# Issuing the second copy of the high query rows on ScalarE's queue

## The reference

```python
def xattn(x, ctx, Wq, bq, Wk, Wv, Wo):        # both layers, in short
    q = (layernorm(x) @ Wq + bq).reshape(b, l, 16, 8)
    k = (ctx @ Wk).reshape(b, m, 16, 8)
    v = (ctx @ Wv).reshape(b, m, 16, 8)
    att = softmax(einsum('blhd,bmhd->blmh', q, k) / sqrt(8), axis=2)
    return einsum('blmh,bmhd->blhd', att, v).reshape(b, l, 128) @ Wo
x = x + xattn(...)                   # layer 0
x = x + quantised_ffn(layernorm(x))
x = x + xattn(...)                   # layer 1
x = x + experts(layernorm(x))        # 8 experts
```

## Time and profile before

| | |
|---|---|
| median of three runs | 409.39 us (409.24 to 411.62) |
| the profiled execution's own span | 411.6 us |
| TensorE matmuls busy | 309.9 us, 75% |
| VectorE busy | 267.8 us, 65% |
| ScalarE busy | 167.3 us, 41% |
| GpSimd busy | 91.0 us, 22% |
| DMA engines | 14.0% on the queue of SP, 0.3% on that of ScalarE |

### The profile page before, as it was taken

One profiled execution on the slowest core, in us unless ns is written; L12 is line 12 of the kernel. 1 busy time (PEld: TensorE's weight loads), 2 busy tenths in 40 slices (PEclk: granted clock), 3 DMA queues, 4 the chain that ended last, 5 costly groups with the idle time before them and its releaser, 6 DMA issues.

```text
span 411.6 us, 4782 instructions
## 1 busy us (share of the span) xinstructions
PE 309.9 (75%) x1455; PEld 184.4 (45%) x1455; DVE 267.8 (65%) x682; ACT 167.3 (41%) x261; POOL 91.0 (22%) x87
## 2 busy tenths in 40 slices
PE   0068689978888843712657698989889999999995
PEld 0046333343434431202234334444437868888883
DVE  1576555367663736985677734766348799988883
ACT  0232152333546313863112334554664445454542
POOL 1511037001010205931110700101010653330600
PEclk9999985589999965855555559999999999999999
DMA  4338421030000091030230200200000000000000
GB/s 143 88 65 175 105 58 28 6 77 2 6 4 5 15 236 40 0 103 2 58 91 7 60 21 14 71 6 2 7 0 2 1 2 25 2 1 25 2 25 25
DMA packets 15902, 16.53 MB, mean 40 GB/s; under 512 B 3435, under 2 KB 11804, under 8 KB 15878
## 3 DMA queue, kind: packets, MB, share of 16 engines
q1 hardware_dynamic: 14834, 13.71, 14.0%
q0 software_dynamic: 704, 2.12, 2.0%
q10 hardware_dynamic: 340, 0.40, 0.3%
HBM read 4.53 MB, written 1.05 MB: 14 GB/s over the span
## 4 chain that ended last, share of the span: by engine, by line
PE 58%; DVE 25%; DMA 6%; ACT 6%; issue 3%; POOL 1%; SPq 0%; ACTq 0%; DVEq 0%; POOLq 0%
PE ps_acc L1092 11%; PE ps_tok L941 6%; PE ps_key L950 5%; DVE mx L645 5%; DMA wkv<-in_wkv 5%; PE ps_acc L1062 4%; PE ps_acc L1064 3%; PE ps_acc L1063 3%; DVE xn L571 3%; DVE stats L561 3%; PE ps_m L958 2%; PE ps_m L980 2%; PE ps_tok L1049 2%; PE ps_tok L1051 2%; DVE axb L849 2%
## 5 line engine op out<-in xcount | busy, mean ns | idle before, releaser
L645 DVE TENSOR_REDUCE mx<-ps_tok 128x4 f32<-128x312 f32 x128 | 57.4, 477 | 38.3 <-PE ps_tok L941 37.4
L441 ACT ACTIVATE big<-ps_key 104x512 f32<-104x512 f32 x96 | 55.3, 596 | 54.1 <-PE ps_key L950 52.8
L941 PE MATMUL ps_tok<-kst,qst 97*128 97x312 f32 x128 | 59.0, 487 | 14.7 <-DVE mx L645 14.2
L334 POOL TENSOR_SCALAR veps<-mv 128x4 f32<-128x4 f32 x16 | 3.7, 229 | 247.8 <-DVE mv L564 247.8
L941 PEld LDWEIGHTS ps_tok<-kst,qst 97*128 97x128 f32 x128 | 30.8, 247 | 52.6 <-DVE mx L645 27.0
L950 PE MATMUL ps_key<-qst,kst 105*104 105x512 f32 x96 | 45.3, 483 | 3.9 <-ACT big L441 1.9
L787 DVE TENSOR_TENSOR qst<-big,qst 128x512 fp32r<-128x512 f32 x64 | 44.3, 692 | 2.2
L785 DVE CAST qst<-big 128x512 fp32r<-128x512 f32 x64 | 27.0, 422 | 9.7 <-ACT big L505 9.5
L571 DVE TENSOR_SCALAR xn<-x,mv,rstd 128x128 f32<-128x128 f32 x64 | 27.5, 595 | 8.8 <-POOL rstd L335 8.8
L505 ACT ACTIVATE big<-ps_tok,b 128x512 f32<-128x512 f32 x32 | 22.0, 689 | 25.1 <-PE ps_tok L1051 24.9
L1092 PE MATMUL ps_acc<-big,vbd 104*32 104x512 f32 x192 | 30.5, 712 | 0.7 <-ACT big L441 0.7
(11 more groups left out here) (192 smaller groups left out, 543.5 us busy)
## 6 DMA issues: line engine op xcount, KB each, us to landing
qst<-qhi SPq DMA_DIRECT2D x64, 64.0 KB, 2.0
kst<-rbuf SPq DMA_DIRECT2D x24, 156.0 KB, 3.0
qst<-qlo SPq DMA_DIRECT2D x32, 64.0 KB, 2.0
w1f<-in_w POOLq DMA_DIRECT2D x2, 1024.0 KB, 7.9
x<-in_x SPq DMA_DIRECT2D x4, 256.0 KB, 10.5
out<-xn SPq DMA_DIRECT2D x4, 256.0 KB, 2.3
qst<-mthl SPq DMA_DIRECT2D x32, 16.0 KB
wqo<-in_wqo SPq DMA_DIRECT2D x1, 256.0 KB, 7.1
```

The costliest lines, as they stand in the source:

```text
L441: act.activation(p[:, j, :], key[n % 2][0:PR, :], ACT.Exp, scale=SCALE).then_inc(q["p_ready"], 1)
L645: nc.vector.tensor_reduce(mx[:, u % 2, t, g, 0, :], tok[n % 2][:, 0:KG].rearrange("p (j h) -> p h j", h=HG), AX.X, ALU.max).then_inc(q["to ...
L941: mm(tok[n % 2][:, 0:KG], qst[0:MASKROW + 1, s, g, 128 * t:128 * t + 128], kst[0:MASKROW + 1, b, g, :], start=True, stop=True).then_inc(q[ ...
```

## The change

The copy of qhi to rows 64 to 95 of the stack is no longer issued by SP but by ScalarE, for all eight units, right behind the ACTIVATE that writes qhi. ScalarE first waits for its own semaphore `q_hi`, and from unit 3 on for `key_put`, as SP does. Sources, destinations, sizes and completion semaphores are the same; SP keeps eight of the twelve DMAs of a unit, ScalarE gets four.

```diff
--- before.py
+++ after.py
@@ -243,6 +243,8 @@
         FIRST_LOG, FIRST_A, FIRST_B, FIRST_C = 5, 6, 8, 12
 
 
+        SECOND_ON_ACT = range(2 * B)
+
         ACT_LATE = dict(copy=0.4, key=0.2)
         DVE_LATE = dict(on=0.1)
 
@@ -301,7 +303,8 @@
                             if u == 0 and g > 0:
                                 key_stack(g)
                             move(qst[0:32, s, g, :], qhi[r, u % 2, :], stack_q[u % 2][g])
-                            move(qst[64:96, s, g, :], qhi[r, u % 2, :], stack_q[u % 2][g])
+                            if u not in SECOND_ON_ACT:
+                                move(qst[64:96, s, g, :], qhi[r, u % 2, :], stack_q[u % 2][g])
                             if g == 0:
                                 sp.wait_ge(q["q_lo"], u + 1)
                             move(qst[32:64, s, g, :], qlo[r, u % 2, :], stack_q[u % 2][g])
@@ -460,6 +463,13 @@
                         if u == B:
                             act.wait_ge(q["const_set"], 5)
                         act.activation(qhi[:, u % 2, :], m1[:, :], ACT.Identity, bias=bq[:, L:L + 1]).then_inc(q["q_hi"], 1)
+                        if u in SECOND_ON_ACT:
+                            act.wait_ge(q["q_hi"], u + 1)
+                            if u >= 3:
+                                act.wait_ge(q["key_put"], 12 * (u - 2))
+                            for g in range(G):
+                                act.dma_start(qst[64:96, u % 3, g, :].bitcast(F32), qhi[32 * g:32 * g + 32, u % 2, :].bitcast(F32)
+                                              ).then_inc(stack_q[u % 2][g], 16)
                     if job == "ot":
                         act.wait_ge(q["ot_put"], u + 1)
                         if u >= 1:
```

## The result

| | before | after |
|---|---|---|
| median | 413.51 us (12 runs, 408.4 to 420.1) | 414.87 us (12 runs, 412.1 to 417.8) |
| ratio, 95% interval | | 1.0099, 1.0052 to 1.0146 |
| span of the profiled execution | 411.6 us | 416.0 us |

The account below looks back on a forecast made before the run. No queue and not ScalarE was taken as the bound; TensorE ended the chain for 58%, VectorE 25%. Costs 0.85 (unit 2) plus 1.3 (unit 7) gave 2.15 us, +0.5%: 409.39 became 411.5 us, range 408.8 to 418.2.

Parts of the forecast that it names:

- SP's relief: SP issues 32 fewer copies, a unit's stack out 2.5 us sooner; gain taken as 0 of at most 0.9 us.
- The price of an issue, 0.63 us: Each of four DMA issues behind qhi on ScalarE takes 0.63 us, blocking ScalarE 2.5 us per unit.
- Units 0, 1, 4 and 5 hidden: ScalarE idles behind qhi there, 4.11 us in unit 4 and longer in the others, so cost 0.
- Unit 2, +0.85 us: Delayed exponential moves a key matmul by 1.8 us; TensorE's idling takes up part, probability matmuls start 0.85 us later.
- Unit 3, 0: Key matmul waits for the delayed exponential, but TensorE had idled 2.46 us for VectorE's rounding of weights: cost 0.
- Unit 6, 0: Two key matmuls are delayed, but TensorE waits 2.92 us for VectorE's line 571 there anyway: cost 0.
- Unit 7, +1.3 us: Two key matmuls wait for delayed exponentials with no TensorE idle time behind them; probability matmuls move by 1.3 us.
- The sum, 2.15 us: Whole kernel: 0.85 us from unit 2 plus 1.3 from unit 7, all else 0; +0.5%.
- the clock apart as a rival: TensorE's clock falls behind unit 7's stall: 413 to 421 us, chance 0.12; unit 2's low stretch shortens: about 406, 0.08.
- the blocked queues: ScalarE's and SP's issues cannot overlap: 4.9 us blocked per unit, 8.75 us together, 418.1 us; chance 0.20.
- issues of 0.9 us or more: Sign on either queue, ScalarE's or SP's, that would make the rival of queues holding each other up.
- Hidden altogether: ScalarE's issues as short as 0.4 us, or unseen idle time eats the stalls: 409.4 us; chance 0.15.

Follow-up runs that it names:

- e8_covered_again: Repeat run of the kernel before with the second qhi copy moved to ScalarE's queue only in units 0, 1, 4 and 5; ratio 1.0003.
- e4_eight: Against the change: ScalarE issues both qhi copies, eight DMAs behind each qhi, and SP only those of qlo; ratio to the kernel before 1.0385.
- e1_covered: Kernel before with the second qhi copy moved to ScalarE's queue only in units 0, 1, 4 and 5; first run, ratio 1.0039.
- e3_late: Against the change: all eight units on ScalarE's queue, but issues of units 2, 3, 6, 7 placed behind exponentials two units earlier; ratio to the kernel before 0.9983.
- e10_only_seven: Kernel before with the second qhi copy moved to ScalarE's queue in unit 7 alone; ratio 1.0061.
- e6_two_seven: Kernel before with the second qhi copy moved to ScalarE's queue in units 2 and 7 alone; ratio 1.0124.
- e2_exposed: Kernel before with the second qhi copy moved to ScalarE's queue only in units 2, 3, 6 and 7; ratio 1.0037.
- e5_held: Kernel before, all DMAs on SP, with four dummy ScalarE writes behind qhi in units 2, 3, 6 and 7; ratio 1.0098.
- e9_only_two: Kernel before with the second qhi copy moved to ScalarE's queue in unit 2 alone; ratio 1.0040.
- e7_change_again: The change as it is, all eight units, measured again against the kernel before; ratio 1.0146.

## Why the prediction was right, and where it was off

- **SP's relief is worth nothing.** Right. The wait that bounded the gain went from 0.9 to 0.7 us, and SP's stack of the second unit, out 3.5 us earlier, made nobody start sooner: e8_covered_again, with the relief in units 0, 1, 4 and 5, is at 1.0003.
- **The price of an issue, 0.63 us.** Too low where both queues issue in step: in units 2 and 7 four took 2.88 us, 0.72 each, and the exponential started 2.95 us after qhi's end, not 2.5. The second and third are the long ones (0.87 and 0.76 us in unit 2). In unit 4, where SP's second issue started 0.4 us behind ScalarE's second instead of 0.2, four took 2.45 us, the price of the forecast, and so did the issues of e4_eight from unit 1 on. The term held for a queue that isn't disturbed; the disturbance, left to a rival, was there in part.
- **Units 0, 1, 4 and 5 hidden.** Right (e8_covered_again), up to 0.1 us in unit 0, whose four issues took 3.86 us.
- **Unit 2, +0.85 us.** Right in mechanism, mis-sized: 1.5 us. The table has pairs from 1.2 to 2.0; the cleanest are the profiles whose key matmuls there took 0.63 us, the time at 1.2 GHz, with 5.53 or 5.54 us without the hold-up (e1_covered, e3_late, e10_only_seven) and 6.99 with it (the change, e6_two_seven). The stall was 0.45 us longer, and the 1.70 us of work behind it were taken from rows at 2.4 GHz; in the changed kernel the key matmul at its head took 0.72 us, not 0.40.
- **Unit 3, 0.** Right to 0.4 us. From qhi to the transposes that wait for VectorE (line 973 before, 983 after) it was 88.16 - 82.99 = 5.17 us, and 5.17 in e2_exposed and 5.18 in e5_held, with the hold-up; but in the changed kernel 89.28 - 83.73 = 5.55 and in its repeat 5.44, where a gap of 0.4 us stood between the last issue and the exponential, past the cover. No run tells where that gap comes from; one of the same length stood behind qhi in the kernel before, where it cost nothing. The 7.6 us to the probability matmul are no price: e3_late, e8_covered_again and e9_only_two, with no hold-up there, have them too. That is the clock, which is at 1.2 GHz behind the pause in some executions and not in others.
- **Unit 6, 0.** Right: 7.13 and 7.14 us in e2_exposed and e7_change_again, as in the kernel before, though the key matmul waited 1.9 us.
- **Unit 7, +1.3 us.** Right, 1.5 us, the rest of it the longer issues.
- **The sum, 2.15 us.** Half of what came: 1.5 + 1.5 = 3.0 us at the two places. Another 1.2 to 2.6 us came behind unit 7 where the clock fell, in four of six profiles, so about 4.3 us or 1.0% on average, an estimate that meets the 1.0099. The weakest step is the one that set the clock apart as a rival with a chance of 0.12. The reason for it was given there, a stretch in which TensorE is busy about 1.1 of 2 us where there was none before; it should have been part of the likeliest case, at about 2 us times two chances in three. The rest of what lacks is the 0.45 us of longer issues, paid twice.
- **The time, 411.5 us, and the range.** That 414.87 lies inside 408.8 to 418.2 says little: the range takes in no loss at all as well as the blocked queues. The forecast's own narrower range, 410 to 413, was missed, by the underrated loss and by the 409.39 that it started from.
- **The rivals.** The two queues do hold each other up, in part, and where it is worst it is hidden. In unit 0 the recorded sign of that rival, issues of 0.9 us or more, is there on both queues: ScalarE's took 0.60, 0.84, 1.25 and 1.07 us, and SP's copy beside them 1.16 where it took 0.60 before. It is so in all six profiles that move unit 0's copies and in none of the six others. In units 2 and 7 the disturbance comes to 0.4 us of 2.88, far from the 4.9 us of the rival, while SP's issues kept their 0.59. What decides which issue is drawn out, and by how much, wasn't tested; it goes with how far apart the two queues' issues start. The Trainium skill (Perfetto Trace Analysis, § DMA Instruction — HWDGE) has each issuing sequencer lock the descriptor generator for itself. The trace doesn't show the alternation that the prediction drew from it: in unit 2 the first issues of both queues start at 55.09 us and take 0.53 and 0.54 us side by side. The rival's price was too low, too: 8.75 us for 4.9 us of hold-up, where e4_eight with 5.0 us cost 15.8, though 2.1 of them in unit 0, held up for 7.5 us, and some by the clock. "Hidden altogether" fell at units 2 and 7.

What stays open: why the clock falls behind the same stall in four profiles and not in two, and whether the stall of unit 2 also moves the end of the long stretch at 1.2 GHz in the first layer. By the recorded clock that ended between 69 and 85 us in four profiles without the stall and between 81 and 87 in five with it (e4_eight apart), so these runs can't tell.

## What to carry to other kernels

A DMA issue is an instruction of the engine that issues it, so it costs what stands behind it there: ask whether the next instruction was already due, not how busy the engine is on average. ScalarE was 41% busy and SP's twelve DMAs for a unit were hardly waited for (0.9 us in all); moving four of them cost about 1%, and moving the same four behind exponentials with slack cost nothing. And where a stall on another engine opens a gap in TensorE's work, price the gap and the granted clock behind it together.

## What the runs showed of the hardware

**An issue can lie under the engine's own work.** With a wait on the ACTIVATE ahead of it, as in the change, an issue starts after that ACTIVATE and holds up the next. Without one, as in e3_late, it starts together with it and is through after 0.51 us of its 0.60. That goes for one issue: where two stand behind one exponential (units 2 and 3), the second ends 0.6 to 1.1 us after it, which costs nothing there because the next exponential comes 1.1 to 3.6 us after it:

```profile
60.04 1.67 ACTq L439 DMA_DIRECT2D qst<-qhi  x2
62.89 0.60 ACT L451 ACTIVATE big<-ps_key 104x512 f32<-104x512 f32 x1 [2.26 <-PE ps_key L969]
```

**VectorE's x normalisation ends 0.86 us after GpSimd is through.** Line 581 (571 before) took 3.96 us in the earlier trace rows and 4.99 in the changed kernel. GpSimd and VectorE there, in the changed kernel:

```profile
233.55 4.99 DVE L581 TENSOR_SCALAR xn<-x,mv,rstd 128x128 f32<-128x128 f32 x4
...
233.17 4.51 POOL L385 TENSOR_TENSOR w2l<-w1f,w2h 128x2048 fp32r<-128x2048 f32 x1
```

It ended 0.85 or 0.86 us after w2l in all twelve profiles (238.54 against 237.68 here, 235.53 against 234.68 before): the first of the four operations ends 0.1 us after w2l, whenever it started, and four such operations take 1.11 us elsewhere. So its length is set by how early it starts under w2l. In three profiles (the change, e6_two_seven, e9_only_two), where the clock had risen just ahead of unit 6, unit 6 came 1.0 us sooner behind unit 5 (21.2 us instead of 22.2) and w2l didn't: it began 1.8 us after unit 6's qhi instead of 0.75, and the interval is 8.15 us instead of 7.13. That took the microsecond back, with the copy on ScalarE or without. What holds VectorE's operation there no run tested.

**The granted clock in the records is not always that of the matmuls.** In e1_covered the windows gave 1.00 for 50 to 85 us, while eight probability matmuls took 1.94 us there, as they do where the clock reads 0.50, and 1.06 later:

```profile
50.00:85.00 35.00, 32.35 (x104) 1.00 0.13 27
...
67.59 1.94 PE L1102 MATMUL ps_acc<-big,vbd 104*32 104x512 f32 x8
```

The durations of one shape are the surer sign.
